# Rows of zeros under the second layer's attention stacks, and the first layer's outputs in two chunks

## What is computed

```python
h = tok_embed(x)                                             # x: (16, 32, 32, 29)
h = h + attn0(layernorm(h))    # group norm, 8 heads of 64, softmax, residual inside
h = h + ffn0(layernorm(h))     # two triangular matrices, gelu
h = h + attn1(layernorm(h))    # 8 heads of 16, softmax
h = h + switch_ffn(layernorm(h))   # 16 experts, top 1, capacity over all images

scores = jnp.einsum('bhqe,bhke->bhqk', Q, K) * scale
attn = jax.nn.softmax(scores, axis=-1)
out = jnp.einsum('bhqk,bhke->bhqe', attn, V)
```

## Time and profile before

| | |
|---|---|
| median of 3 runs | 8411.39 us (8378.32 to 8422.72) |
| the profiled execution | 8371.84 us |
| its span, first to last instruction | 8370.1 us |
| mean granted TensorE clock | 0.833 |
| PE / PEld busy | 88% / 51% |
| DVE / ACT / POOL busy | 60% / 38% / 21% |
| DMA, mean of the span | 37 GB/s |

### The profile page before, as it was taken

One profiled execution on the slowest core, in us unless ns is written; L12 is line 12 of the kernel. 1 busy time (PEld: TensorE's weight loads), 2 busy tenths in 40 slices (PEclk: granted clock), 3 DMA queues, 4 the chain that ended last, 5 costly groups with the idle time before them and its releaser, 6 DMA issues.

```text
span 8370.1 us, 124378 instructions
## 1 busy us (share of the span) xinstructions
PE 7405.4 (88%) x39399; PEld 4297.5 (51%) x39399; DVE 5002.4 (60%) x11545; ACT 3213.9 (38%) x6291; POOL 1774.3 (21%) x1623
## 2 busy tenths in 40 slices
PE   6798998989989899898988989899898998989987
PEld 4555555545545455454555545555554555545532
DVE  5664665656666565565656656566565665656554
ACT  3343443433434343343433434334343443434431
POOL 2322222222222222222221222222222221222200
PEclk8887897988988878798887888879788787888866
DMA  2220211111121110211102111111111111111000
GB/s 63 47 47 20 49 32 40 39 43 36 26 49 39 33 39 23 49 39 33 39 22 52 37 43 39 29 43 29 43 39 41 31 32 43 38 40 39 22 24 7
DMA packets 89184, 308.91 MB, mean 37 GB/s; under 512 B 23942, under 2 KB 30022, under 8 KB 78278
## 3 DMA queue, kind: packets, MB, share of 16 engines
q1 hardware_dynamic: 88518, 300.53, 15.6%
HBM read 49.33 MB, written 41.94 MB: 11 GB/s over the span
## 4 chain that ended last, share of the span: by engine, by line
issue 63%; POOL 17%; PE 14%; DVE 4%; DMA 1%; POOLq 0%; SPq 0%; ACT 0%; DVEq 0%; ACTq 0%
POOL pr_lo L456 9%; POOL on L1183 3%; PE bank L776 3%; PE bank L749 2%; POOL on L1175 2%; PE bank L735 2%; PE bank L792 1%; PE bank L806 1%; PE bank L793 1%; PE bank L774 1%; DVE hm L1448 1%; DMA stacks<-parts 1%; DVE mxh L1458 1%; POOL h L1153 1%; PE bank L816 1%
## 5 line engine op out<-in xcount | busy, mean ns | idle before, releaser
L1458 DVE TENSOR_REDUCE mxh<-bank 128x1 f32<-128x512 f32 x4096 | 2761.3, 689 | 2300.8 <-PE bank L749 2275.4
L1029 ACT ACTIVATE pr<-bank 128x512 f32<-128x512 f32 x4096 | 2400.1, 598 | 3343.0 <-PE bank L776 3276.2
L749 PE MATMUL bank<-stacks 128*128 128x512 f32 (+1 forms) x4096 | 2036.1, 508 | 403.3 <-DVE mxh L1458 369.6
L776 PE MATMUL bank<-stacks 65*128 65x512 f32 (+1 forms) x4096 | 1929.2, 482 | 5.7 <-ACT pr L1029 5.7
L749 PEld LDWEIGHTS bank<-stacks 128*128 128x128 f32 (+1 forms) x4096 | 862.8, 214 | 1088.0 <-DVE mxh L1458 791.0
L456 POOL TENSOR_TENSOR pr_lo<-pr 128x1024 bf16<-128x1024 f32 x496 | 940.1, 1895 | 1933.7 <-ACT pr L1029 1933.7
L792 PE MATMUL bank<-v,pr 128*128 128x129 bf16 x8192 | 1308.1, 251 | 7.5 <-DVE pr_lo L456 5.1
L793 PE MATMUL bank<-v,pr_lo 128*128 128x129 bf16 x7936 | 1272.2, 251 | 0.0
L776 PEld LDWEIGHTS bank<-stacks 65*128 65x128 f32 (+1 forms) x4096 | 839.5, 210 | 767.7 <-issue 609.6
L774 PE MATMUL bank<-stacks 128*128 128x512 f32 x2048 | 1049.8, 513 | 47.0 <-issue 40.8
L792 PEld LDWEIGHTS bank<-v,pr 128*128 128x128 bf16 x8192 | 904.1, 113 | 357.1 <-issue 338.7
(11 more groups left out here) (180 smaller groups left out, 5209.8 us busy)
## 6 DMA issues: line engine op xcount, KB each, us to landing
stacks<-parts SPq DMA_DIRECT2D x384, 512.0 KB, 6.7
parts_d<-pr SPq DMA_DIRECT2D x16, 2048.0 KB, 6.5
stacks<-parts_d SPq DMA_DIRECT2D x224, 128.0 KB
stacks<-parts_d SPq DMA_DIRECT2D x224, 64.0 KB
stacks<-mrow SPq DMA_DIRECT2D x512, 2.0 KB
out<-hm SPq DMA_DIRECT2D x16, 512.0 KB, 2.7
stacks<-pr SPq DMA_DIRECT2D x32, 128.0 KB
stacks<-pr SPq DMA_DIRECT2D x32, 64.0 KB
```

The source lines that it names most:

```text
L749: mm(maxb[k % 2][:, :], qs[:, t * P:(t + 1) * P], ks[:, g * HALF:(g + 1) * HALF], start=True, stop=True).then_inc(max_filled.sem, 1)
L776: mm(bank[:, :], k_stack(layer, head)[0:last, kk], q_stack(layer, head)[0:last, q], start=(layer == 1), stop=True).then_inc(score_filled.s ...
L1029: act.activation(pr[:, at % 2, kt, :], score[k % 2][:, :], ACT.Exp, scale=SCALES[layer]).then_inc(exp_done.sem, 1)
L1458: dve.tensor_reduce(mxh[:, layer, n // 2, n % 2:n % 2 + 1], maxb[k % 2][:, :], AX_X, ALU.max)\
```

## The change

`stacks1` gets 128 partitions for each of its two heads in place of 64. All of it is filled with zeros once; the key stacks' row 48 is set to ones once, by two DMAs that SP waits for before it loads the first image. The second layer's max tiles and scores contract all 128 rows. Since a max tile now also reads row 48, in which the query stack would hold the maxima of an earlier head, the fifth DMA of a stack's load no longer writes ones to the keys but copies a row of zeros (row 127) over the queries' row 48. To make room, `on` has 256 columns in place of 512: heads 0 to 3 and 4 to 7 use the same places, and VectorE waits, before the first write of heads 4 and 6, until the transposes of the chunk that was there have been drained. The tables of steps are the same, and the order of matmuls on PE is the same.

```diff
-        stacks1 = sb("stacks1", [P, 2, S], F32R)
+        stacks1 = sb("stacks1", [P, 2, 2, S], F32R)
-        on = sb("on", [P, T, INNER])
+        on = sb("on", [P, T, 2 * P])
...
         def k_stack(layer, head):
-            return kB[:, head % 2] if layer == 0 else stacks1[64 * (head % 2):64 * (head % 2) + 64, 0, :]
+            return kB[:, head % 2] if layer == 0 else stacks1[:, head % 2, 0, :]
...
             sp.wait_ge(prep_dve, PREP_DVE)
+            for n in range(2):
+                sp.dma_start(stacks1[3 * D1:3 * D1 + 1, n, 0, :].rearrange("a (t q) -> a t q", t=T).bitcast(F32), ones[0:T, :])\
+                    .then_inc(ones_in, 16)
+            sp.wait_ge(ones_in, 32)
...
                                (kk[2 * D1:3 * D1], src[a:b_, 1, :]), (qq[2 * D1:3 * D1], src[a:b_, 3, :]),
-                               (kk[3 * D1:3 * D1 + 1].rearrange("a (t q) -> a t q", t=T), ones[0:T, :])])
+                               (qq[3 * D1:3 * D1 + 1], qq[P - 1:P])])
...
-                turn(seg, f"oT0.{c}.{g}", lambda j: on[:, 4 * g + j, c * P:(c + 1) * P])
+                turn(seg, f"oT0.{c}.{g}", lambda j: on[:, 4 * g + j, c % 2 * P:(c % 2 + 1) * P])
...
-                    qs, ks = q_stack(1, head)[0:3 * D1], k_stack(1, head)[0:3 * D1]
+                    qs, ks = q_stack(1, head), k_stack(1, head)
...
-                last = max_row(layer) + 1
+                last = max_row(0) + 1 if layer == 0 else P
...
+            dve.memset(stacks1[:, :, :, :].bitcast(F32), 0.0)
...
                     dve.wait_ge(on_ready.sem, on_ready.at(seg.l0, own - 3))
+                if u in (8, 12) and jj == 0:
+
+                    await_drained(dve, seg, f"oT0.{u // 4 - 2}.0", f"oT0.{u // 4 - 2}.1")
```

More of the change, by code:

```diff
@@ L382, in build @@
         prep_pool = sem("prep_pool")
+        ones_in = sem("ones_in")
         x_loaded = Counts(sem("x_loaded"), 16)
@@ L463, in k_stack @@
         def k_stack(layer, head):
-            return kB[:, head % 2] if layer == 0 else stacks1[64 * (head % 2):64 * (head % 2) + 64, 0, :]
+            return kB[:, head % 2] if layer == 0 else stacks1[:, head % 2, 0, :]
         def q_stack(layer, head):
-            return qB[:, head % 2] if layer == 0 else stacks1[64 * (head % 2):64 * (head % 2) + 64, 1, :]
+            return qB[:, head % 2] if layer == 0 else stacks1[:, head % 2, 1, :]
         def max_row(layer):
@@ L1173, in normalize0 @@
                 pool.wait_ge(o_drained.sem, o_drained.at(seg, o_place(seg.kind, 0, u, jj) + 1))
-                o = on[:, t:t + 2, head * D0:(head + 1) * D0]
+                o = on[:, t:t + 2, head % 4 * D0:(head % 4 + 1) * D0]
                 pool.tensor_tensor(o, o, o_r[:, n % 4, :].unsqueeze(2).broadcast_to([P, 2, D0]), ALU.mult)\
@@ L1481, in outputs0 @@
                     dve.wait_ge(on_ready.sem, on_ready.at(seg.l0, own - 3))
+                if u in (8, 12) and jj == 0:
+                    await_drained(dve, seg, f"oT0.{u // 4 - 2}.0", f"oT0.{u // 4 - 2}.1")
                 dve.reciprocal(o_r[:, own % 4, :], bank[:, :, 2 * D0])
-                dve.tensor_tensor(on[:, t:t + 2, head * D0:(head + 1) * D0], bank[:, :, D0:2 * D0],
+                dve.tensor_tensor(on[:, t:t + 2, head % 4 * D0:(head % 4 + 1) * D0], bank[:, :, D0:2 * D0],
                                   o_hi[:, own % 2, :, 0:D0], ALU.add).then_inc(o_drained.sem, 1)
```

## The result

The changed kernel takes **7486.6 us** (median of 4 runs, 7476 to 7493), against 8403.5 us for the kernel before in the same set of runs; the ratio is 0.891 with a 95% interval of 0.888 to 0.894. The forecast was 7,800 us, with a range from 7,525. The profiled execution took 7493.2 us with a span of 7491.4; against the profiled 8371.8 us before that is a gain of 879 us (917 between the medians), where the sum of the forecast had 602.

What follows compares the result with a forecast made beforehand. PE was taken as the limiter, its clock down in the second layer's few-row matmuls. Gains 490 (clock) + 45 (last units) + 70 (PE's own time) - 3 (startup) = 602 us off 8371.8, scaled to the median: 7,800 us, range 7,525 to 8,170.

Steps and rivals of the forecast that it cites:

- How much low time goes: Time at 1.2 GHz in the second layer's units: 1,560 us, of which 90%, 1,400 us, was to go.
- the end: Last 16 units, second layer alone: half of 194 us at 1.2 GHz goes at 0.45, 45 us gained.
- What a microsecond of it is worth: Second-layer units: each microsecond no longer at 1.2 GHz gains 0.35 us, so 1,400 us give 490 us.
- second pair of rows 8: One second-layer unit in two turns, 15.38 us against 14.61: 0.77 us for 3.3 us low, 0.23 each.
- first pair: Another second-layer unit in two turns, 17.73 us at 0.90 against 16.22 at 1.00: 0.43 per low microsecond.
- PE's own time: Second layer's matmuls: form changes save 265 us, lost simultaneous starts cost 130; about half on the path, 70 us gained.
- The entry: Going into a second-layer short form costs 0.09 us extra, about 8 times a unit.
- The exit: Coming out of a short form to a 128-row tile costs 0.19 us extra, about 2 times a unit.
- The lost pairs: Second-layer score and next head's tile no longer start together: 0.24 us each, 540 pairs, 130 us of PE lost.
- The chain beside PE: Rival: PE's tiles wait for VectorE's reductions once the clock is up, price 0.2, 8,110 us; chance 0.16.
- The clock answers to zero rows: Against the rival that it doesn't, or goes by busy time: 8,340 us, or 8,411 if even; chance 0.09.
- The pairs: Rival: clock stays and lost simultaneous starts of second-layer score and tile cost 130 + 3 us, 8,545 us; chance 0.06.

Runs made afterwards that it cites:

- the two runs that padded more rows elsewhere: Changed kernel with the experts' biases at 128 rows: 7431 us; changed kernel with the first layer's second score matmul at 128 rows: 7407 us.
- all three kernels shown: Changed kernel with 16-row biases (7487 us), with biases at 128 rows (7431 us), and with first-layer scores at 128 rows, biases still 16 (7407 us).

## Why the prediction was partly right and where it failed

**What bounds the kernel, and why the clock is down: right.** PE was the limiter, the short matmuls of the second layer were what let its clock fall, and zero rows count as rows. The low time falls by 917 us from 65 through 96 to 128 rows, with the form and the length of a unit at full clock unchanged, and by 341 us more with the first layer's scores at 128 rows; ones in place of zeros change nothing. Rows are not the whole rule: with tiles alone padded the last segment stayed at 0.50, and why is open.

**How much low time goes: right.** Forecast 1,400 us in the attention and half of the end's 194, 1,497 in all, measured 1,522. That the sums lie so close is partly luck: the second layer's units gave 1,255 (84% and not 90% of theirs), the end 155 where 97 were forecast, and the first layer's units 82 that were not counted.

**What a microsecond of it is worth: wrong, and the largest miss.** The step was "Between the two I take 0.35". The forecast had 490 us from it and, at 0.45, 45 for the end, 535 together; at the 0.49 that the runs from 65 to 128 rows gave, 1,522 us are about 750. The low end of the pair was read wrongly. In the second pair of rows 8 both turns still had a low stretch: 0.23 is the price of a second one on top of the first. Taking away the last one gives 0.48 in the same unit. Removing both is nearer the first pair's 0.43 than their mean, and my own reason ("because the whole of the low time goes") should have excluded the lower figure. That reason does not hold everywhere, though: in the two runs that padded more rows elsewhere, the low time that was left went for about 0.3.

**PE's own time: right in kind, too small.** The entry was put at 0.09 us from one distance; behind the experts it is 0.20, because the tile behind the score pays too, and the way back to the values costs another 0.09, which was not counted. The exit was put at 0.19 against a neighbour distance of 0.24 that does not hold there (0.32) and is 0.12. The engine time per unit came out near (1.1 against 1.5), but the factor of one half for the path was wrong in this unit: 1.34 us show in its length at full clock. First-layer units gain as well, 0.31 us each in the 203 that are at 1.00 with 64 and with 65 rows, which the sum left out. From 64 to 65 rows the profiled time falls by 375 us; less the 270 us of low time at 0.49, the forms are worth some 240 us, where 265 x 1/2 had been counted. That split is worked out: 1.33 us in each of 240 units and 0.31 in the first layer's would be more than the whole 375, so a unit with low time cannot gain both in full.

**The lost pairs: right in kind.** 130 us of PE, half on the path, against 182 and 146 measured. Much of that may be the clock: low time grew by 264 us in one and by 165 in the other, which at 0.49 would leave 53 and 65 us, near the 65 counted. That split is worked out, not measured.

**The sum of it:** clock 750, forms 240, pairs and start 55 lost: 935 us, against 879 between the two profiled executions. The parts are priced at one rate and overlap, and the remaining 56 us stay open; the smaller price among short forms (0.39) would take back more than half of them. Of the 277 us by which the 602 fell short, some 215 are the clock's price and low time and some 110 the forms, before these 56 are taken off.

**The rest: right.** The chunks and VectorE's waits cost nothing, the start 3.2 us (3 forecast), the stacks' loads show nothing, the serial part is nearly as it was (97.7 us against 100.4). The last segment, "some 45", is 60.

**The rivals.** The chain beside PE did not bind: the price is 0.49 and not 0.2. The clock answers to zero rows. The pairs are real but small beside the rest: 182 and 146 us. The Trainium skill ("TensorE: Matmul & The Clock Gate", Part 3, The mechanism) has matmuls in different row groups run at once; the trace agrees, with equal starts at 2003.65. Around the expert biases PE is counted busy 3.60 of 3.60 us in all three kernels shown, and the clock falls behind them in one and stays up in the two with more rows. The same page's Part 1 speaks of how busy PE has been and not of rows; here the measurement goes beyond it.

## What to carry to other kernels

When TensorE is the limiter and its granted clock is down in a stretch in which it is busy, look at how many rows its matmuls contract. Here rows of zeros cost no time in the matmul (15.01 us a unit with 96 and with 128) and held the clock up, and a row more than 64 took matmuls out of a short form whose weights were loaded late at a change (1.33 us a unit). Pad neighbours together, since half of them padded was worth less than a third. Price a microsecond of low clock by the same unit with and without any, not with more and less of it, and expect the price to differ by place: 0.49 here, about 0.3 for what was left.

## What was not expected

One added row, from 64 to 65, was worth 373 us of 8327 (4.5%) with the clock nearly the same (0.852 and 0.862). Padding the tiles alone made the last segment slower than with no padding in the same layout (325.8 against 304.7 us), with the clock at 0.50 throughout. And the first layer's 65-row scores, in a stretch that already showed 1.00 in most units, still gave 80 us when padded to 128. Between the profiled executions it is 91 us for 341 us less at 1.2 GHz, 0.27 us each, little more than half the price found before; 207 of the 341 lie in the second layer's units, whose matmuls were not touched. Why it is less was not tried.
